# The routed experts of an adaLN block, unrolled with a skew of three tiles; softmax totals inverted one key tile later

## What is computed

```python
h = _layernorm(x) * (1 + ca) + sa
x = x + ga * attention(h)        # 32 heads of 8, 8 key/value heads, causal, softmax
h = _layernorm(x) * (1 + cb) + sb
x = x + gb * ffn(h)
```

```python
for e in range(16):
    g, u = split(h @ up_w[e].T)              # 256 -> 2 x 176
    out += cw[:, e:e+1] * ((silu(g) * u) @ down_w[e].T)   # 176 -> 256
out += swiglu(h @ shared_up_w.T) @ shared_down_w.T
```

## Time and profile before

| | before |
|---|---|
| median of 3 runs | 803.39 us (802.52 to 803.60) |
| profiled execution, own time | 799.27 us |
| its span | 797.5 us |
| TensorE busy | 671.5 us, 84% |
| VectorE busy | 423.8 us, 53% |
| ScalarE busy | 330.5 us, 41% |
| GpSimd busy | 342.0 us, 43% |
| attention's scores to the last value product | about 103 to 413 us |
| expert loop, first row load to last down product | 527.5 to 769.5 us |

### The profile page before, as it was taken

The page is one execution under the profiler, slowest core; times in us unless marked ns, Lnnn a source line. Parts: engine busy times, 40 slices in busy tenths (PEclk is TensorE's granted clock), DMA queues, the critical chain, the costliest instruction groups (busy, mean ns, idle before and its releaser), DMA issues.

```text
span 797.5 us, 12808 instructions
## 1 busy us (share of the span) xinstructions
PE 671.5 (84%) x3356; PEld 353.9 (44%) x3357; DVE 423.8 (53%) x872; ACT 330.5 (41%) x752; POOL 342.0 (43%) x438
## 2 busy tenths in 40 slices
PE   3965799998989998999879998739999999899950
PEld 3532343433433443344117455515666566565630
DVE  5513857676766776667426698503333333333327
ACT  2440046676565656565662332103333333333310
POOL 4241144525252524253320757724555555455540
PEclk9997559999998999899685998959999999999985
DMA  6166520444141414020207933834555556555548
GB/s 218 44 136 176 139 92 2 91 166 98 36 88 35 89 38 85 14 47 3 45 0 240 340 113 140 262 93 76 95 90 94 88 95 95 83 94 94 88 64 292
DMA packets 65462, 83.30 MB, mean 104 GB/s; under 512 B 11660, under 2 KB 58220, under 8 KB 64688
## 3 DMA queue, kind: packets, MB, share of 16 engines
q1 hardware_dynamic: 48800, 61.41, 28.3%
q0 software_dynamic: 14448, 19.31, 14.8%
q10 hardware_dynamic: 2176, 2.10, 0.8%
HBM read 47.63 MB, written 34.77 MB: 103 GB/s over the span
## 4 chain that ended last, share of the span: by engine, by line
PE 42%; DMA 26%; DVE 8%; ACT 7%; issue 7%; POOL 6%; SPq 2%; POOLq 0%; DVEq 0%; ACTq 0%
DMA y_sum<-arena,token_no 13%; PE bank L607 9%; PE bank L596 6%; POOL x_rows L1149 6%; ACT arena L944 5%; DMA y_totals<-arena 5%; PE bank L582 5%; PE bank L822 5%; PE bank L839 3%; PE bank L719 3%; PE bank L586 2%; DMA arena<-k_parts 2%; DVE arena L1466 2%; DMA mod_rows<-arena 1%; PE bank L625 1%
## 5 line engine op out<-in xcount | busy, mean ns | idle before, releaser
L1210 DVE TENSOR_REDUCE negm<-bank 128x2 f32<-128x1024 f32 (+3 forms) x176 | 191.2, 1119 | 95.4 <-PE bank L586 95.0
L944 ACT ACTIVATE arena<-bank 128x512 f32<-128x512 f32 x320 | 180.1, 599 | 115.7 <-PE bank L596 113.0
L1157 POOL DMA_INDIRECT y_sum<-arena,token_no x79 | 123.0, 1557 | 124.2 <-DVE arena L1466 115.6
L1072 POOL TENSOR_SCALAR_AFFINE_SELECT arena<-arena 128x512 f32<-128x512 f32 x128 | 79.9, 639 | 158.1 <-ACT arena L944 154.8
L582 PE MATMUL bank<-arena 72*128 72x512 bf16 (+3 forms) x512 | 124.1, 325 | 23.1 <-DMA arena<-k_parts 15.0
L596 PE MATMUL bank<-arena 75*128 75x512 bf16 x320 | 123.9, 405 | 14.3 <-ACT arena L944 9.1
L822 PE MATMUL bank<-arena 128*128 x316 | 116.4, 492 | 1.1 <-issue 1.1
L1455 DVE CAST token_no<-arena 128x1 uint32<-128x1 f32 x79 | 12.1, 154 | 150.5 <-DMA y_sum<-arena,token_no 132.6
L586 PE MATMUL bank<-mask_qk,ident_bf 128*128 128x128 bf16 (+2 forms) x352 | 92.1, 262 | 0.0
L607 PE MATMUL bank<-arena 128*32 128x512 f32 x640 | 87.8, 661 | 4.1 <-ACT arena L933 4.1
L1149 POOL DMA_INDIRECT x_rows<-arena,slots x64 | 63.7, 995 | 43.1 <-DVE slots L1365 24.2
(11 more groups left out here) (170 smaller groups left out, 719.3 us busy)
## 6 DMA issues: line engine op xcount, KB each, us to landing
arena<-x_rows SPq DMA_DIRECT2D x79, 136.5 KB, 2.5
arena<-q_parts SPq DMA_DIRECT2D x24, 384.0 KB
arena<-up_t SPq DMA_DIRECT2D x2, 2816.0 KB, 16.6
arena<-y_sum SPq DMA_DIRECT2D x8, 512.0 KB, 6.6
q_parts<-arena SPq DMA_DIRECT2D x4, 768.0 KB, 5.8
x_rows<-arena SPq DMA_DIRECT2D x17, 136.5 KB, 2.9
arena<-k_parts SPq DMA_DIRECT2D x24, 96.0 KB
y_sum<-arena SPq DMA_DIRECT2D x1, 2176.0 KB, 7.6
```

The source lines that it names most:

```text
L944: nc.scalar.activation(probs[:, group % SLOTS, g, :], bank[:, 4 + tile % 2, :], ACT.Exp, scale=SCALE).then_inc(s["st_free"], 1)
L1072: nc.gpsimd.affine_select(out=block_, in_=block_, compare_op=ALU.is_ge, fill=0.0, base=0, pattern=[[0, REP], [1, P]], channel_multiplier=- ...
L1157: gp.indirect_dma_start(y_sum[i % 2], bass.IndirectOffsetOnAxis(ap=token_no[i % STEPS][:, :], axis=0), yo[i % STEPS], None, compute_op=ALU ...
L1210: nc.vector.tensor_reduce(to, view, AX.X, ALU.max, negate=True).then_inc(s["s_free"], 1)
```

## The change

- The expert loop has no hardware loops and no credits: 79 tiles written out, waits on constants (through `above`, which leaves out a wait for a count of zero or less). The expert's number is still read into a register for each tile.
- `xt` has eight buffers. Token number and weight are read by the scatter and by the weighing straight from the buffer; the token number is stored as an integer in the row. `extras` and its buffers are gone. SP's load of tile t+8 waits for scatter t.
- The skew is three tiles: TensorE does up of t+1, row transposes of t+3, activation transposes of t, down of t-1. ScalarE and VectorE follow that order. The weighing waits for the scatter four tiles back (`yo` keeps four buffers).
- The inner size is split into 88 and 88 instead of 128 and 48: both transposes and both down matmuls have 88 rows, one copy on ScalarE takes both pieces, nothing needs zeros, and `wd_zero`, the memset and the credits' memsets are gone.
- In attention, `invert` moves from (4, 3) to (5, 2), `normalise` from (8, 0) to (8, 2), `project` and `residual` from (8, 3) and (9, 1) to (9, 1) and (9, 3).

```diff
+XT, YO = 8, 4
+I2 = I // 2
...
-                            if u > 0 and (n, g) == (4, 3):
+                            if u > 0 and (n, g) == (5, 2):
                                 invert(u - 1)
-                            if u > 0 and (n, g) == (8, 0):
+                            if u > 0 and (n, g) == (8, 2):
                                 normalise(u - 1)
-                            if u % 2 == 0 and u > 0 and (n, g) in ((8, 3), (9, 1)):
-                                residual(u // 2 - 1, int(n == 9))
+                            if u % 2 == 0 and u > 0 and (n, g) in ((9, 1), (9, 3)):
+                                residual(u // 2 - 1, g // 2)
...
-                def one(t, i, more, far):
-
-                    sp.wait_ge(s["tx_done"], 2 + t + 1)
-                    sp.nop(nofuse=True)
-                    sp.wait_ge(s["extra"], t + 1)
-                    load(t + STEPS, i)
...
+                for t in range(TILES):
+                    if t >= XT:
+                        sp.wait_ge(scat[t % 2], 16 * ((t - XT) // 2 + 1))
+                    load(t)
...
+                for t in range(3):
+                    turn_rows(t)
+                expert = {0: expert_of(0)}
+                up(0, expert[0])
+                for t in range(TILES + 1):
+                    if t + 1 < TILES:
+                        expert[t + 1] = expert_of(t + 1)
+                        up(t + 1, expert[t + 1])
+                    if t + 3 < TILES:
+                        turn_rows(t + 3)
+                    if t < TILES:
+                        turn_act(t)
+                    if t > 0:
+                        down(t - 1, expert.pop(t - 1))
...
-                    nc.scalar.activation(actT[i % 2][:, 0, :], bank[:, 4 + i % 2, 0:P], ACT.Copy)
-                    nc.scalar.activation(actT[i % 2][0:I1, 1, :], bank[0:I1, 4 + i % 2, P:2 * P],
+                    above(act, s["dn_done"], t - 1)
+                    nc.scalar.activation(actT[t % 2][0:I2].rearrange("p c n -> p (c n)"), bank[0:I2, 4 + t % 2, 0:2 * P],
                                          ACT.Copy).then_inc(s["aT_ready"], 1)
...
+                for t in range(TILES):
+                    if t + 1 < TILES:
+                        silu(t + 1)
+                    if t + 3 < TILES:
+                        rows_out_of_psum(t + 3)
+                    act_out_of_psum(t)
...
+                def add_rows(t):
+                    gp.wait_ge(s["yo_ready"], t + 1)
+                    above(gp, scat[t % 2], 16 * (t // 2))
+                    gp.indirect_dma_start(y_sum[t % 2],
+                                          bass.IndirectOffsetOnAxis(ap=xt[t % XT][:, D:D + 1].bitcast(U32), axis=0),
+                                          yo[t % YO], None, compute_op=ALU.add).then_inc(scat[t % 2], 16)
...
-                        extras(t + 2, i + 2, 16 * trip + 16 * ((i + 2) // STEPS) + 16,
-                               32 * trip + 16 * ((i + 2) // 2) - 16)
-                        gated(t + 1, i + 1)
-                        weigh(t, i)
...
+                def weigh(t):
+                    e = dve.value_load(tile_expert[0:1, t:t + 1], min_val=0, max_val=E - 1)
+                    dve.wait_ge(s["dn_done"], t + 1)
+                    above(dve, scat[t % 2], 16 * ((t - YO) // 2 + 1))
+                    nc.vector.tensor_scalar(yo[t % YO], bank[:, 6 + t % 2, 0:D], xt[t % XT][:, bass.ds(e + D + 1, 1)],
+                                            None, ALU.mult).then_inc(s["yo_ready"], 1)
...
+                gated(0)
+                for t in range(TILES + 1):
+                    if t + 1 < TILES:
+                        gated(t + 1)
+                    if t > 0:
+                        weigh(t - 1)
```

More of the change, by code:

```diff
@@ L203, in adaln_block @@
         tab = sb("tab", [1, 3, TILES])
-        token_no = [sb(f"token_no{i}", [P, 1], U32) for i in range(4)]
-        weight = [sb(f"weight{i}", [P, 1]) for i in range(4)]
         names = """norm2 y_mm added norm_st norm_mv centred inverse_sd w_in wm_in wg_in c_in wo_in
@@ L1049, in _ @@
-                over_tiles(act, one)
+                rows_out_of_psum(0)
+                rows_out_of_psum(1)
+                silu(0)
+                rows_out_of_psum(2)
+                for t in range(TILES):
[4 more added lines that the diff above has]
+                    act_out_of_psum(t)
             @block.gpsimd
```

192 lines of the change are left out of this document (47 added, 145 removed).

## The result

| | before | after |
|---|---|---|
| median | 802.95 us (802.14 to 803.60) | 761.95 us (761.36 to 765.81) |
| profiled execution, own time | 799.27 us | 761.93 us |
| its span | 797.5 us | 760.1 us |
| TensorE / VectorE busy | 671.5 / 423.8 us | 646.9 / 408.4 us |
| ScalarE / GpSimd busy | 330.5 / 342.0 us | 318.3 / 338.9 us |

The times before are those of the runs made beside the changed kernel. The ratio is 0.950, with an interval of 0.947 to 0.953: 41 us less, against a forecast of 766 us and 37 us less.

The account below looks back on a forecast made before the run. The prediction took VectorE's copies waiting for scatters to bound the expert loop. Loop 26 us plus attention 11 us gave 37 us less, 766 us from a median of 803.39; range 755 to 786 us.

Parts of the forecast that it names:

- the ring: Expert loop before the change: VectorE's token-number copy waits for a scatter and delays later gating; 2.86 us per tile.
- TensorE's floor: Expert loop: TensorE alone needs 2.49 us per tile; as a rival, loop at that pace, 758 us, chance 0.25.
- the ring through the row buffers: Changed expert loop: load of tile t+8 waits for scatter t; 9.85 us over four tiles, 2.46 us per tile.
- the pace of 2.60 us: Expert loop: 0.55 us added for scatters and loads slowing each other, 10.4 us over four tiles.
- any stretch of a transfer shows: Expert loop: without reserve, slower transfers lengthen the pace; both expected stretches together give 2.83 us per tile.
- scatters landing later than 3.84: Expert loop, a sign of the forecast being right: scatters take longer than 3.84 us from start to landing.
- Start: Loop's beginning: a third pair of transposes moves the first up product from 532.32 to about 533.5 us.
- End: Loop's end: the last three scatters come closer than their parity chain allows, giving back 2 us.
- 7.7 + 2 x 1.7: Attention: VectorE's waits for the totals plus slowed value products in two halves, a gain of 11 us.
- Value products of 1.85 us in every half: Attention, a sign of the forecast being right: sixteen value products take 1.85 us, where two halves showed 3.57.
- The pace staying: Expert loop rival: row-buffer waits keep the old pace, needing 11.9 us over four tiles; 794 us, chance 0.07.
- the slower case: Expert loop rival: transfers in flight together slow each other much more, 3.51 us per tile; 835 us, chance 0.05.

Follow-up runs that it names:

- six buffers: The changed kernel with six row buffers for the loaded rows instead of eight: 969.91 us, ratio 1.164 to the kernel before.
- ten and twelve: The changed kernel with ten or twelve row buffers instead of eight: 780.65 us with ten, 783.21 us with twelve, beside 833.79 for the kernel before.
- the experiment: The changed kernel with only attention's inversion moved back to (4, 3): 797.59 us, beside 781.92 us for the changed kernel.
- the second execution of the changed kernel: The changed kernel measured again with nothing altered, in a later group: 781.92 us, ratio 0.946 to the kernel before.
- a loop of TensorE without the larger blocks: The changed kernel with TensorE's tiles 8 to 71 as a hardware loop of eight tiles a turn, other engines unrolled: 790.82 us.
- the kernel meant to have half as many again: The changed kernel with 16 empty instructions per tile written into TensorE's stream, which did not reach the program: 789.06 us.

## Why the prediction was right, and where it was off

**What bounded the loop:** right. The copies' wait on the scatter of four tiles back was the ring, its removal brought the pace from 2.97 to near TensorE's floor, and the next bound is the ring through the row buffers. Its length, 9.85 us, was confirmed by six buffers (9.7 to 10.0), though two of its terms were off and cancelled. Its want of reserve was confirmed by ten and twelve, where the late loads no longer reached TensorE.

**The term that was off: the pace of 2.60 us.** The forecast spread 0.55 us over every ring, as scatters and loads slowing each other steadily. That did not happen. Most tiles ran at 2.49, and the loss came as seven single stalls of 1.05 to 1.55 us, six of late loads and one of a lower clock, which the forecast had at nothing. That the mean came near 2.60 is luck: it was (202.3 - 1.9) / 76 = 2.64 in the profiled execution, and (194.4 - 1.9) / 76 = 2.53 in the second. The forecast had "any stretch of a transfer shows" right and, as far as the runs go, the source of the stretch wrong: it looked among the data transfers, and left out a third user of the DMA queues, the fetched instructions of an unrolled loop. The landings of the loads and of the scatters in the changed kernel:

```profile
DMA to landing us min/median/max: 2.1/2.5/4.3
```

```profile
DMA to landing us min/median/max: 3.7/3.8/4.9
```

Scatters took 3.8 us in the median, as in the rows of before, so the sign "scatters landing later than 3.84" did not come. But 4.7 is not the first scatter's alone, and 3.1 not the longest load: single scatters up to 4.9 us and loads up to 4.3 stand in the loop.

**Start:** the third pair of transposes cost 0.9 us: up(0) starts at 520.4 instead of 532.3, 11.9 earlier, where the last scatter into x_rows starts 12.8 earlier (511.3 against 524.1). The forecast said 1.2. The clock was better than assumed: 0.84 on average from 520 to 530 us (the window above) and not 0.50 during two ups, so that tile 0 was weighed at 527.8 and not at 530.8, half of which is attention's larger gain.

**End:** 2 us given back, as counted.

**Attention:** right in kind, 11 forecast, 12.3 measured and 14.6 in the experiment. The sum 7.7 + 2 x 1.7 was VectorE's waits plus the two value products. What TensorE gained is its own wait for the maxima, 8.1 - 1.6 = 6.5 us, and 3.4 in the value products; for the 2.4 us that are left the forecast had a candidate in its upper bound of 13, the other matmuls slowed in those stretches, and no run tells them apart. Five waits went as forecast; the sixth, in the last half, grew from 2.3 to 4.2 us, not down to 0.5, and is off the chain. "Value products of 1.85 us in every half" missed the last half, where 3.3 to 3.6 us stand before and after.

**The sum:** 41 measured, 37 forecast, 26 + 11. The last weighing was forecast for 741.3 - 11 = 730.3 and came at 730.05; the two errors, 3.0 us of a start that came too early for the forecast and 2.8 us of a loop that took longer, cancel nearly, which is luck. What the median has beyond it is not a term: the profiled execution's own time was 762 forecast and 761.93 measured, and the median lies at 761.95 with it this time, not 4 us above.

**The rivals.** TensorE's floor was near: in the second execution of the changed kernel the loop was 3 us from it. The pace staying and the slower case needed a ring of 11.9 or 12.4 us in the mean; 9.7 to 10.0 was measured. The Trainium skill's floor of 600 ns for a register load (DMA: Bandwidth & Descriptors, Latency and other measured facts) would, as an estimate from the page, have made the ring 0.33 us longer; the register loads of the changed kernel took 0.27 us in the median, so the trace doesn't agree. The Trainium skill's 2 us for an HBM access at high load (same page and section) did not show at a DMA share of 0.66 either: loads landed in 2.5 us in the median as before.

**What stays open:** what exactly makes a load late. A block of code is in flight with every late load, and a loop of TensorE without the larger blocks had no stall over 1 us, but one execution had the blocks and no stall, and the kernel meant to have half as many again did not get them. Open too is why the clock fell behind one late load and not behind the others.

## What to carry to other kernels

Add up the ring of every buffer that is freed at a far end (here scatter, landing, sync, load, the work up to the next scatter) and divide by the tiles it spans. Where that comes within a few per cent of the engine's floor, it isn't a pace to be averaged but a ring without reserve: one or two more buffers, or one tile less of skew, cost nothing here and kept rare late transfers from reaching the engine; one of the two was enough. And a wait of an off-path engine ahead of work that TensorE needs costs more than its own length, if TensorE's clock falls meanwhile: move the waiting instruction past what is already there to be done.

## What the runs showed of the hardware

- **A weight piece of 48 rows between pieces of 128:** in these float32 matmuls the step from 128 rows to 48 and the step back each left 0.33 us idle before the weight load, 0.39 us per tile together and 19.9 us in the kernel's time (809.00 against 789.06). The steps from 128 to 88 rows and back in the changed kernel left none.
- **An unrolled loop uses the DMA engines:** one 16 KB block of instructions took 1.4 us of one engine; 30 blocks and 28 smaller ones in this kernel, 20 and 18 before. Loads in flight with one landed in 2.9 us in the median and up to 4.3, the others in at most 3.0.
- **TensorE's clock behind a stall:** after 1.29 us of idle time at 588.3 to 589.6 us the granted clock was 0.50 from 591.4 to 594.8 us, and an up took 2.59 us instead of 1.35. After the five other stalls of this trace, with 0.9 to 1.2 us, it stayed at 1.00, and so it did after 1.32 us in the kernel with the inversion put back.
- **A turn of a hardware loop** on TensorE cost 0.76 to 1.02 us here, once in eight tiles.
- **A register load** from SBUF took 0.27 us on SP in the median, in the kernel before and in the changed one.
